# Second attention and second experts in one block, with part of the second experts' preparation moved into the attention

## What is computed

```
x = x + xattn0(LN(x), ctx)          # similarity attention
x = x + experts0(LN(x))             # top 2 of 12 (4 of them zero-cost), silu, hidden 512
x = x + xattn1(LN(x), ctx, mask)    # 4 heads of 64, 1024 keys per batch, mask, then @ Wo
x = x + experts1(LN(x))             # below

# experts1, xf = LN(x) as 2048 rows
logits = xf @ Wg                                  # 8 experts
top_vals, top_idx = top_k(logits, 2);  gate = softmax(top_vals)
comb = one_hot(top_idx) . gate * alpha
for e in range(8):
    hdn = layernorm(xf, ln_w[e], ln_b[e])
    a = gelu(hdn @ fc1_w[e] + fc1_b[e]);  y = a @ fc2_w[e] + fc2_b[e]    # 256 -> 1024 -> 256
    out = out + y * comb[:, e:e+1]
```

## Time and profile before

| | |
|---|---|
| median of 3 runs | 962.05 us (961.77 to 968.83) |
| the profiled execution's own time | 967.79 us |
| its span in the profile | 965.9 us |
| mean granted clock of PE | 0.956 |
| instructions | 19473 |
| mean DMA rate | 139 GB/s |

### The profile page before, as it was taken

How to read it: one execution, slowest core, us unless ns; L and a number is a source line. 1 busy time by engine, 2 the same in 40 slices (tenths; PEclk the granted TensorE clock), 3 DMA queues, 4 the chain that set the end, 5 groups by cost and what they waited for, 6 DMA issues and landing times. The chain is left out here.

```text
span 965.9 us, 19473 instructions
## 1 busy us (share of the span) xinstructions
PE 894.5 (93%) x6189; PEld 766.2 (79%) x6190; DVE 562.0 (58%) x1286; ACT 491.3 (51%) x1044; POOL 431.3 (45%) x374
## 2 busy tenths in 40 slices
PE   6899999868999998779999999988899999999995
PEld 4798989746899996557777777757499999999995
DVE  7875453485566675666566575554764454454452
ACT  5744141354444553475665665545655455455552
POOL 2474341004555573755363462300255555555543
PEclk9999999978999999789999999985999999999998
DMA  9721000275766746611010100019667666676662
GB/s 306 239 95 44 1 1 1 76 248 187 254 228 232 253 157 221 135 44 44 5 63 22 45 1 2 28 52 353 229 184 195 211 200 190 209 203 187 206 198 28
DMA packets 68593, 134.72 MB, mean 139 GB/s; under 512 B 8080, under 2 KB 50704, under 8 KB 63408
## 3 DMA queue, kind: packets, MB, share of 16 engines
q1 hardware_dynamic: 55184, 110.27, 33.4%
q0 software_dynamic: 13344, 23.63, 11.2%
HBM read 109.08 MB, written 21.64 MB: 135 GB/s over the span
## 5 line engine op out<-in xcount | busy, mean ns | idle before, releaser
L1901 PEld LDWEIGHTS d_hps<-d_xg_t,d_xw 128*128 128x128 f32 x1248 | 145.2, 192 | 2.4 <-DVE d_xg_t L2085 1.0
L1799 ACT ACTIVATE x<-d_hps,b 128x128 f32<-128x128 f32 x312 | 89.3, 368 | 113.1 <-PE d_hps L1901 112.9
L1901 PE MATMUL d_hps<-d_xg_t,d_xw 128*128 128x128 f32 x1248 | 145.5, 275 | 0.8 <-DVE d_xg_t L2085 0.8
L883 POOL TENSOR_SCALAR c_prob<-c_prob,c_rinv 128x1024 f32<-128x1024 f32 x64 | 72.4, 1150 | 109.4 <-DVE c_rinv L1338 109.0
L1911 PE MATMUL d_yps<-d_w,d_hid_hi 128*128 x312 | 115.2, 402 | 0.0
L1704 POOL DMA_INDIRECT out_x<-d_y,d_take_slot x39 | 63.1, 1619 | 99.1 <-DVE d_y L2122 89.6
L1331 DVE CUSTOM_DVE_ANT_0 c_prob<-c_sc,c_minf 128x1024 f32<-128x1024 f32 x64 | 75.8, 1221 | 36.6 <-PE c_sc L976 34.4
L2085 DVE TENSOR_SCALAR d_xg_t<-d_take,ln_w,ln_b 128x128 f32<-128x128 f32 x78 | 28.5, 406 | 93.4 <-PE d_take L1890 93.1
L1914 PE MATMUL d_yps<-d_w,d_hid_lo 128*128 x312 | 81.2, 281 | 0.0
L1901 PEld LDWEIGHTS b_hps<-b_xg_t,b_w 128*128 128x128 f32 x624 | 76.7, 195 | 3.6 <-issue 1.9
L989 PE MATMUL c_tp<-const,c_prob 128*128 128x128 f32 x512 | 70.5, 281 | 9.8 <-DVE c_pt L1343 5.2
(11 more groups left out here) (367 smaller groups left out, 2106.6 us busy)
## 6 DMA issues: line engine op xcount, KB each, us to landing
d_xw<-in_w SPq DMA_DIRECT2D x39, 1024.0 KB
b_w<-in_w SPq DMA_DIRECT2D x47, 512.0 KB, 7.6
d_w<-in_w SPq DMA_DIRECT2D x8, 1024.0 KB, 12.3
a_raw<-in_ctx_t SPq DMA_DIRECT2D x8, 512.0 KB, 7.0
a_raw<-in_ctx SPq DMA_DIRECT2D x8, 512.0 KB, 4.6
ybuf<-a_zero SPq DMA_DIRECT2D x2, 2048.0 KB, 12.5
k_stage<-in_ctx_t SPq DMA_DIRECT2D x12, 256.0 KB, 3.0
rows<-b_xn_all SPq DMA_DIRECT2D x1, 2048.0 KB, 12.6
```

Source lines behind the costliest of these rows:

```text
L883: nc.gpsimd.tensor_scalar(prob[w][:], prob[w][:], rinv[:, w:w + 1], 1.0, ALU.mult, ALU.mult).then_inc(s["prob_ready"], 1)
L1799: op = nc.scalar.activation(hid[q][:, h * FH + c, :], src[:, c, :], ACT.Gelu_apprx_tanh, bias=b1[:, ds(e, 1), h * FH + c])
L1901: mm = nc.tensor.matmul(hps[j % 2][h][:, c * P:(c + 1) * P], w1[j % WL][:, k, at:at + P], xg_t[j % 2][:, k, :], start=(k == 0), stop=(k == ...
```

## The change

The first experts, the second attention and the second experts are three programs of one block: SP, PE, ACT, DVE and POOL each go from one list into the next without a boundary. The second experts' tiles and semaphores are allocated first, and stay beside those of the attention. With that, work of the second experts is written into the attention:

- SP loads w2 of experts 2 and 3 in batch 1, of 0 and 1 when the last values are formed, of 4 (with gw and alpha) after the last maxima; then it waits for twelve normalised tiles and sends them to `rows`, then loads w2 of 5, 6, 7 (`early_rows`, LAST_LOW). The last four tiles follow in the experts' own list.
- w2 of experts 2 and 3 is split in four halves of 128x1024: the high parts by ACT (`early_high`, at HIGH_AFTER, in batches 1 and 2), the low parts by POOL (`early_low`, at EARLY_AT, in batches 1 to 3).
- ACT takes the high halves of experts 0 and 1 in front of the last `keep_heads`; POOL forms their low halves behind its last scaling (`later_low`). DVE keeps 4 and 5, PE 6 and 7; DVE_LAST and LOW_LATE are empty in layer 1.
- The statistics of batch 2 and the variance and square root of twelve tiles move a little ahead; DVE normalises five tiles before its last `keep_second` and seven after the first `add_projection`, and takes the last batch's statistics in two halves around the last addition. ACT normalises no tile.
- In the experts' list, PE's five warm products at the start are gone in layer 1, the turns of pairs 6 and 7 both stand at i == 6, and `value_parts` stands behind the low_out of both PE experts.
- Many semaphores are merged to make room: `routed` and `act_routed` count several events. In layer 0 the eight w2 loads share four semaphores, so `high(e)` waits for both loads of a pair.

The diff, cut to its core:

```diff
+EARLY_LOW = (2, 3)
+LATER_LOW = (0, 1)
+FREE_FIRST = 4
+LAST_LOW = (5, 6, 7)
...
+HIGH_ORDER = (0, 1, 4, 5, 6, 7)
...
+        EARLY_AT = ((1, 2), (2, 0), (2, 2), (3, 0))
+        HIGH_AFTER = ((1, 1), (1, 7), (2, 1), (2, 7))
...
                     out_rows(b - 2)
+                else:
+                    sp.wait_ge(s["sum_p"], 2 * TB * (B - 1))
+                    for n in EARLY_LOW:
+                        m.load_w2(sp, n)
+            sp.wait_ge(s["v_done"], B * 4)
+            for n in LATER_LOW:
+                m.load_w2(sp, n)
             out_rows(B - 2)
             sp.dma_start(dram["out"][T * P:(T + 1) * P, :], m.x[:, 0, :]).then_inc(m.out_ready, 16)
+            sp.wait_ge(s["max_done"], B * UP * 2)
+            m.load_w2(sp, FREE_FIRST)
+            m.early_rows(sp)
+            sp.wait_ge(s["av_done"], B * 4)
+            for n in LAST_LOW:
+                m.load_w2(sp, n)
             out_rows(B - 1)
...
                     normal(b, u)
+                    if (b, u) in EARLY_AT:
+                        m.early_low(pool, EARLY_AT.index((b, u)))
...
+            for n in LATER_LOW:
+                m.later_low(pool, n)
...
                 keep_first(b, 0, 1)
+                if (b, 1) in HIGH_AFTER:
+                    m.early_high(act, HIGH_AFTER.index((b, 1)))
...
             keep_first(B - 1, 7, 0)
+            root(0, B - 1, 21)
             keep_heads(B - 1, 2)
             keep_first(B - 1, 7, 1)
+            for n in LATER_LOW:
+                m.high(act, n)
             keep_heads(B - 1, 3)
-            root(0, B - 1, 21)
...
+            def half_stats(half):
+                dve.wait_ge(s["x_ready"], B * 2 - 1 + half)
+                for t in range(T - TB + 2 * half, T - TB + 2 * half + 2):
+                    op = nc.vector.bn_stats(m.bn[:, t, :], m.x[:, t, :])
+                op.then_inc(s["x_bn"], 1)
...
                 keep_second(b, 4, 1)
+                if not more:
+                    new_stats(b - 1)
...
                 keep_second(b, 5, 1)
+                if not more:
+                    dve.wait_ge(s["x_bn"], 2 * B - 1)
+                    variance(nc, m, dve, s["stat"], cols(0, B - 1), 15)
...
+                if before and more:
                     new_stats(b - 1)
 
             keep_second(B - 1, 7, 0)
+            dve.wait_ge(s["v_done"], B * 4)
+            inverse_std(nc, m, dve, s["stat"], s["sqrt_done"], cols(0, B - 1), 15, 3)
+            m.early_normal(dve, 0, 5)
             keep_second(B - 1, 7, 1)
-            dve.wait_ge(s["x_bn"], 2 * B - 1)
-            variance(nc, m, dve, s["stat"], cols(0, B - 1), 15)
-            late_scale(0, B - 1, 15, 3)
             add_projection(B - 1, 0, xb)
+            m.early_normal(dve, 5, T - TB)
+            half_stats(0)
             add_projection(B - 1, 1, tp[1])
-
+            half_stats(1)
...
-    ACT_TILES = 4
+    ACT_TILES = 4 if first else 0
+    XN_OUT = 32 if first else 48
...
-    DVE_LOW, PE_LOW, DVE_LAST = ((0, 1, 2, 3), (4, 5), (6, 7)) if first else ((0, 1), (2, 3, 4), (5, 6, 7))
-    HIGH_AT = (1, 3, 5, 7) if first else (3, 5)
-    LOW_LATE = PE_LOW[len(PE_LOW):] if first else PE_LOW[-1:]
+    DVE_LOW, PE_LOW, DVE_LAST = ((0, 1, 2, 3), (4, 5), (6, 7)) if first else ((4, 5), (6, 7), ())
+    HIGH_AT = (1, 3, 5, 7) if first else (4, 5)
...
-        w2_in = [sem(f"w2_in{e}") for e in range(E)]
-        gate_in = [sem(f"gate_in{q}") for q in range(LANES)]
+        w2_in = [sem(f"w2_in{e}") for e in range(E // 2 if first else E)]
...
+        def high(act, e):
+            if first:
+                act.wait_ge(w2_in[e // 2], 32)
+            else:
+                act.wait_ge(w2_in[e], 16)
+            nc.scalar.activation(w2[:, e, :, 0, :], w2[:, e, :, 1, :].bitcast(F32), ACT.Copy).then_inc(s["w2_hi"], 1)
+        def high_count(e):
+            return e + 1 if first else HIGH_ORDER.index(e) + 1
...
+        def early_normal(dve, lo, hi):
+            for t in range(lo, hi):
+                normalise(nc, m, xn_all[:, t, :], t).then_inc(s["xn_dve"], 1)
+        def early_rows(sp):
+            sp.dma_start(gw[:], dram["gate_1"].rearrange("(k p) e -> p k e", p=P)).then_inc(s["w_in"], 16)
+            sp.dma_start(alpha[:], dram["alpha"].partition_broadcast(P)).then_inc(s["w_in"], 16)
+            sp.wait_ge(s["xn_dve"], T - TB)
+            sp.dma_start(dram["rows"][0:(T - TB) * P, :].rearrange("(t p) d -> p t d", p=P),
+                         xn_all[:, 0:T - TB, :]).then_inc(s["xn_out"], 16)
+            sp.dma_start(dram["rows"][T * P:(T + LANES) * P, :].rearrange("(t p) d -> p t d", p=P),
+                         xn_all[:, 0:LANES, :]).then_inc(s["xn_out"], 16)
...
-            for e in PE_LOW[:2]:
+                                     bias=m.const[:, C_ONES:C_ONES + 1]).then_inc(s["act_routed"], 1)
+            for e in PE_LOW:
                 low_out(e)
-                if e == (PE_LOW[1] if first else PE_LOW[0]):
+                if e == PE_LOW[1]:
                     value_parts()
             for e in DVE_LAST:
-                high(e)
-            for e in LOW_LATE:
-                low_out(e)
...
-            warm(5, rank)
+            if first:
+                warm(5, rank)
             for i in range(AHEAD):
                 turn_pair(i)
             pe.wait_ge(s["w_in"], 32)
             for i in range(PAIRS):
-                if i + AHEAD < PAIRS:
+                if i + AHEAD < (PAIRS if first else PAIRS - AHEAD):
                     turn_pair(i + AHEAD)
+                if not first and i == PAIRS - AHEAD:
+                    for late in range(i, PAIRS):
+                        turn_pair(late)
                 logits(i)
...
-                if e not in LOW_LATE:
-                    low_parts(e)
-
-            pe.wait_ge(s["val_ready"], 1)
-            pe.wait_ge(s["val0_ready"], 1)
+                low_parts(e)
...
-            for e in LOW_LATE:
-                low_parts(e)
             warm(8, rank)
...
-            if not first:
-                weights_low(DVE_LAST[0])
             take_in(0, 0)
             take_in(1, 1)
-            for e in DVE_LAST[0 if first else 1:]:
+            for e in DVE_LAST:
...
+        with nc.cleanup_on_exit():
+            last = experts(nc, m, dram, 1)
+            with ExitStack() as kept:
...
+                @block.sync
+                def _(sp):
+                    first.sync(sp)
+                    second.sync(sp)
+                    last.sync(sp)
...
```

More of the change, by code:

```diff
@@ L33 @@
 LANES = 3
+EARLY_LOW = (2, 3)
+LATER_LOW = (0, 1)
+FREE_FIRST = 4
+LAST_LOW = (5, 6, 7)
+ROUTED = {n: k + 1 for k, n in enumerate("load exp_in expert blk val slot g gate_at".split())}
+ACT_ROUTED = {n: k + 1 for k, n in enumerate("exp_ready val0_ready off_ready lane_act".split())}
+HIGH_ORDER = (0, 1, 4, 5, 6, 7)
 GATHERS = 6
@@ L741, in attention1 @@
         wq_hi, wq_lo = (a[:, 6, :].rearrange("p (k d) -> p k d", k=KD) for a in (m.split_hi, m.split_lo))
+        y_late = [[sb(f"y{b}_{k}", [P, TB, D]) for k in range(2)] for b in (2, 3)]
+        sb("gap", [P, 5248])
         q_hi, q_lo = (sb(f"q_{p}", [P, KD, S], F32R) for p in ("hi", "lo"))
@@ L748, in attention1 @@
         att_odd = sb("att_odd", [P, 2 * P])
-        y_late = [[sb(f"y{b}_{k}", [P, TB, D]) for k in range(2)] for b in (2, 3)]
-        sb("gap", [P, 5248])
         wo = sb("wo", [P, KD, D])
@@ L1501, in experts @@
         c16 = lambda at, n: m.c16[:, at - C_ONES:at - C_ONES + n]
+        if not first:
+            xw = sb("xw", [P, T * D])
         w2 = sb("w2", [P, E, FC, 2, D], F32R)
@@ L1613, in run @@
+        if not first:
+            m.load_w2, m.high, m.early_high, m.early_low, m.later_low = load_w2, high, early_high, early_low, later_low
+            m.early_normal, m.early_rows = early_normal, early_rows
         def run(eng, step):
@@ L1727, in scalar @@
             act.sem_inc(s["w2_lo_act"], 2)
-            def high(e):
-                act.wait_ge(w2_in[e], 16)
-                nc.scalar.activation(w2[:, e, :, 0, :], w2[:, e, :, 1, :].bitcast(F32), ACT.Copy).then_inc(s["w2_hi"], 1)
             def low_out(e):
@@ L1940, in step @@
                     pe.wait_ge(s["w2_lo_act"], len(PE_LOW) * CH + 2)
+                    if not first:
+                        pe.wait_ge(s["w2_lo_pool"], 2 * len(EARLY_LOW) + len(LATER_LOW))
                 down(n, j, e)
```

211 lines of the change are left out of this document (114 added, 97 removed).

## The result

The changed kernel takes 970.57 us (median of 17 runs, 968.06 to 973.62), the kernel before 961.77 in the same comparison (17 runs, 958.13 to 971.86). The ratio is 1.009 with a 95% interval of 1.007 to 1.011: slower by 8.8 us, where 4.0 us less was forecast, and outside the range. The profiled execution took 969.88 us with a span of 968.1, 2.2 more than the 965.9 of before. So two questions stand: where the 2.2 come from, and where the other 6.6, which the two profiles don't show.

The account below looks back on a forecast made before the run. TensorE, busy 93% of the span, was taken as the bound. First product 5.4 us earlier, less 1.4 lost in the first experts, gave 4.0: median 962.05 to 958.0 us, range 949.5 to 965.

Parts of the forecast that it names:

- Part 1: Attention: the POOL and ACT work added there fits into idle time, price 0, bounds 0 and 13.2 us.
- Part 2 and 3: Second experts' start: boundary gone, at best 12.7 us; POOL holds DVE's normalising, PE waits, clock falls, so gain 4.7.
- my 666.0: Forecast end of the second experts' logits, against 670.74 before: gain 4.7 us, bounds 0 and 12.7.
- two limits: Second experts' logits end: late tiles with PE at clock 0.50 give 666.0; ACT's wait for expert 5's weights gives 664.5.
- the row's 2.39: Longest hold of DVE by a POOL instruction seen in the earlier profile, 2.39 us; the skill's rule implied 4.8 for double-size subtractions.
- Part 4: Logits to first block, second experts: take_slot loses 1.3 us, the gather gains 3.3, the clock in the first products costs 1.3.
- Part 5: First experts: ACT's first high copy also waits for the second weight load; loss 1.4 us, bounds 0 and 1.5.
- part 3: Second experts' tiles: DVE stands still while POOL subtracts, PE waits, clock taken at 0.50; logits end 666.0, gain 4.7 us.
- the best case: Rival: POOL's subtractions hardly stop DVE's normalising, logits end at 658, gain 12.0 us, 950.0; chance 0.25.
- the attention pays: Rival: ACT's and POOL's added work in batches 1 to 3 pushes PE, full price 13.2 us, 971.3; chance 0.10.

Follow-up runs that it names:

- own_signals: The changed kernel, but each of the eight w2 loads in the first experts has its own semaphore; 964.47 us, ratio 1.0046.
- pool_late: The changed kernel, but POOL's two large subtractions wait until all sixteen tiles are normalised; 966.89 us, ratio 1.0068.
- cold and hot starts: Kernel before, its five warm products at the second experts' start replaced by a wait for four tiles (cold, 966.55 us) or raised to 20 (hot, 963.78 us).
- pairs_warm: Kernel before with the paired w2 signals, plus eight warm products ahead of the third pair's logits in the first experts; 967.64 us, ratio 1.0054.
- tuned runs: Changed kernel with separate load signals, POOL's subtractions apart (954.97 us); plus val's first half earlier and 22 warm products before gathered rows (953.10); these also in first experts (952.05).
- before_hot: Kernel before with 20 instead of 5 warm products at the start of the second experts; 963.78 us, ratio 1.0014.

## Why the prediction was wrong

**Part 1, work in the attention at 0: right.** The stretch from the first experts' last copy to the last c_av got no longer. The hold of POOL on DVE does not touch DVE work that reads PSUM, as the earlier trace rows said.

**Part 2 and 3, the boundary and the hold: right in mechanism, a little off in size.** The seven normalisations took 10.54 us where I had 11.4 (638.3 to 649.7), PE's wait fell at the pair foretold, the clock fell, and expert 5's weights came late. From the last c_av to the logits' copy it took 26.7 us; by my 666.0 it would have been 25.1 (666.0 - 640.9). The gain was 3.1 and not 4.7. I had set two limits side by side, the tiles with PE at 0.50, and ACT's wait for expert 5 with two pairs behind it "even at full clock". They meet in the last two pairs: these stand behind ACT's wait and run at 0.50, 3.8 us (668.45 to 672.27) where I had 2.1 (664.5 - 662.4). How fast the pairs ahead of that wait run doesn't count, and it was from them that the forecast took its end: in own_signals they ran faster, PE waited 3.23 us for ACT and not 2.12, and the copy stands 26.6 behind the last c_av all the same. So POOL's hold costs through the rows and weights that leave late (in pool_late the copy is 20.5 behind the last c_av), and hardly through the clock of the early pairs. The Trainium skill's rule (SBUF — State Buffer, "Who interferes with whom"), a lock held for the whole instruction, was the right reading against the row's 2.39: 4606 and 2447 ns beside instructions of 4.5 and 2.4 us.

**Part 4: right.** take_slot lost 1.3 (21.1 us behind the logits against 19.8), the first product gained 3.3 (5.8 behind take_slot against 9.0). The clock cost 1.9 in the first products and not 1.3: it stayed at 0.50 for some 4 us of them, to about 703, and not for the 2.5 of the first experts, from which I had the term.

**Part 5, the paired signals at 1.4, "bounds 0 and 1.5": this is the step that failed.** It costs 6.4 us alone in the kernel before, and 6.1 (4.7 against the kernel before of each batch) and 8.3 where it was given back in two versions of the change. I had priced the wait and not what it does to the clock, although part 3 did just that for the same kind of wait 450 us later, and although the profile of before showed the first experts' clock on the edge of falling. In the profile: 5.8 us at the logits, 1.41 of them wait. Filling the wait with warm products brought the logits' copy back to 1.2 us behind that of before (15.8 against 14.6, from the stage's start). The upper bound should have been the wait and, behind it, six pairs at the lower level, four with a turn at 1.4 us each (half of the 2.76 of the earlier trace rows) and two without at 0.95: near 9, and not 1.5.

**The profiled run was no typical one.** I wrote that it lay 5.7 above the median and then took the gain "from the median", as if the 5.7 were spread evenly. Most of it sits in the very stage that the change works on: the profile of before has the second experts' logits at 0.50 throughout, an execution of the same code in another kernel shows them 9.3 us earlier and the first product 6.7 us earlier, and the mean clocks of the 101 executions and the cold and hot starts fit a kernel that goes the shorter way in about two of three. So most executions already had what the forecast found there: 5.4 us up to the first product, against 6.7. By profiles the change costs 2.2 us; by medians 8.8.

The sum with what was measured, from the forecast's -4.0 to the span's +2.2: paired signals 5.4 and not 1.4, +4.0; attention 0.7 shorter, -0.7; logits +1.6; first products +0.6; the blocks behind them +0.7; together 6.2.

And against a kernel before that takes the shorter course, as pairs_warm shows it behind the attention: first experts +5.4, attention -0.7, from the last c_av to the first down product +3.6 (62.9 against 59.3 us), the rest +0.7: 9.0, where the medians say 8.8. That both agree so closely is in part luck, since the shorter course stands on one trace, and the mean clock of an execution doesn't name the stage. The first attention varies too: the first experts begin between 183.5 and 185.9 us in the fourteen profiles, and at 185.3 in both of before.

Of the rivals, the best case needed both faults gone and is where the tuned runs ended (952 to 955); "the attention pays" was the only one on the slower side, and had the wrong mechanism.

## What to carry to other kernels

A wait of one or two microseconds on TensorE among light products can cost several times its length: put into the upper bound what the clock does behind it, to the end of the stage, and don't make such a wait for the sake of a few semaphores. Large GpSimd instructions over SBUF belong where VectorE reads PSUM or rests, and moving them needs a look at what they collide with next. Before a gain is read from one profile, ask whether that execution stands at the median, and if not, in which stage it differs: a second profile of the same kernel may show the same course again, but the mean granted clocks of all executions tell whether there are two.

## What was not expected of the hardware

The clock behind PE's gap of 3.3 us at the block's end takes two courses with the same code: at 0.50 for 34 us, or back at 1.00 after some 4 us (0.50 in 648 to 650, 1.00 from 652). Before it rose in before_hot, PE had run warm products for some 4 us; while it ran turned tiles and gate products without a gap, from 649 to 670 in both profiles of before, it did not rise; but in pairs_warm it rose near 651, when five warm products and then turned tiles had run since 647. Nor does the same wait always bring it down: behind 1.48 us for tiles 6 and 7 it fell at once in the change, behind 1.49 us in own_signals some three microseconds later. What decides between the courses stays open. And two engines that hold each other off can both lose: POOL's two subtractions took 11.07 us instead of 9.07 while DVE's two took 10.99 instead of 4.6.
